# A fused attention and feed-forward kernel: the exponents' matmuls at the end of a step, and the transposes of y behind the last of them

## What is computed

```python
x = x + xattn(layernorm(x), ctx, ctx, Wq, bq, Wk, bk, Wv, bv)   # softmax attention on the context
x = x + attn(layernorm(x), Wq, Wk, Wv, Wo, W_feat)              # causal linear attention, 16 heads of 64
x = x + ffn(layernorm(x), w1, w2)                               # quantised linear, gelu, quantised linear

# attn: phi(v) = exp(v @ W_feat - |v|^2/2) / sqrt(128), 128 features
# y_t = sum_{s<=t} (phi(q_t).phi(k_s)) v_s / (sum_{s<=t} phi(q_t).phi(k_s) + 1e-6);  out = y @ Wo
# ffn: activations are rounded to 8 bits by row, weights to -1, 0, 1
```

## Time and profile before

| | us |
|---|---|
| median of 3 runs | 253.53 |
| lowest and highest | 253.51, 253.79 |
| the profiled execution | 253.28 |
| its span, first to last instruction | 251.5 |
| TensorE busy in the span | 239.7 |
| VectorE busy | 187.6 |
| ScalarE busy | 146.5 |
| GpSimd busy | 101.6 |

### The profile page before, as it was taken

The page is one execution under the profiler, slowest core; times in us unless marked ns, Lnnn a source line. Parts: engine busy times, 40 slices in busy tenths (PEclk is TensorE's granted clock), DMA queues, the critical chain, the costliest instruction groups (busy, mean ns, idle before and its releaser), DMA issues.

```text
span 251.5 us, 6988 instructions
## 1 busy us (share of the span) xinstructions
PE 239.7 (95%) x2722; PEld 188.8 (75%) x2728; DVE 187.6 (75%) x476; ACT 146.5 (58%) x284; POOL 101.6 (40%) x139
## 2 busy tenths in 40 slices
PE   7998889999999999999999999999999989999984
PEld 7854556777788778787777878777789978888863
DVE  5577888666742685777888888775688979999994
ACT  0554454534446888567656766765647257787772
POOL 2063113342202558344674578726720024444430
PEclk9999999999999999999999999999999999999999
DMA  7999999990079001100110000000000000000001
GB/s 189 357 390 404 398 395 393 344 390 33 1 252 330 4 0 46 44 3 1 44 44 3 1 3 3 3 0 3 4 3 3 4 0 3 21 23 21 22 26 63
DMA packets 15377, 26.83 MB, mean 107 GB/s; under 512 B 1232, under 2 KB 8688, under 8 KB 15344
## 3 DMA queue, kind: packets, MB, share of 16 engines
q1 hardware_dynamic: 14576, 25.96, 28.9%
q10 hardware_dynamic: 768, 0.43, 0.6%
HBM read 25.33 MB, written 1.05 MB: 105 GB/s over the span
## 4 chain that ended last, share of the span: by engine, by line
PE 63%; DVE 18%; issue 6%; POOL 5%; ACT 4%; DMA 2%; SPq 0%; DVEq 0%; POOLq 0%; ACTq 0%
PE b L1346 11%; PE b L1106 7%; PE b L1390 6%; PE b L1108 6%; PE b L1107 6%; PE b L1365 4%; PE b L1267 3%; PE b L1270 2%; PE b L1263 2%; DMA xwk<-in_xWk 2%; PE b L1520 2%; DVE yT_lo L980 2%; DVE xn L742 2%; PE b L1218 2%; PE b L1186 2%
## 5 line engine op out<-in xcount | busy, mean ns | idle before, releaser
L852 DVE TENSOR_TENSOR x_lo<-b,x_hi 128x512 fp32r<-128x512 f32 x32 | 21.7, 688 | 16.8 <-ACT x_hi L463 16.7
L600 ACT ACTIVATE phi<-b 128x512 f32<-128x512 f32 x48 | 26.0, 597 | 11.3 <-PE b L1346 11.3
L403 POOL TENSOR_TENSOR sq_lo<-sq_sum,sq_hi 128x512 fp32r<-128x512 f32 x16 | 20.6, 1287 | 25.8 <-ACT sq_hi L463 25.8
L345 POOL TENSOR_TENSOR lnr<-lnv,mh 128x1 f32<-128x1 f32 x16 | 8.8, 552 | 54.9 <-DVE lnv L716 54.7
L521 ACT ACTIVATE sq<-b 128x512 f32<-128x512 f32 x32 | 19.3, 603 | 18.1 <-PE b L1108 18.1
L397 POOL TENSOR_TENSOR sq_sum<-sq,sq 128x512 f32<-128x512 f32 x16 | 20.7, 1293 | 21.6 <-ACT sq L521 21.6
L1106 PE MATMUL b<-nT_lo,wp_hi 128*128 128x512 f32 x64 | 26.8, 418 | 0.1
L1108 PE MATMUL b<-nT_hi,wp_hi 128*128 128x512 f32 x64 | 25.0, 391 | 0.0
L1107 PE MATMUL b<-nT_hi,wp_lo 128*128 128x512 f32 x64 | 25.0, 390 | 0.0
L926 DVE TENSOR_TENSOR smk<-b,mask 64x512 f32<-64x512 f32 x32 | 22.0, 688 | 2.9 <-PE b L1365 1.2
L1390 PEld LDWEIGHTS b<-va,smk 128*64 128x64 f32 x512 | 17.5, 137 | 7.5 <-issue 7.1
(11 more groups left out here) (180 smaller groups left out, 615.9 us busy)
## 6 DMA issues: line engine op xcount, KB each, us to landing
cT<-in_ctxT SPq DMA_DIRECT2D x8, 1028.0 KB, 14.0
cn<-in_ctx SPq DMA_DIRECT2D x8, 1024.0 KB, 14.7
wv_raw<-in_aWv SPq DMA_DIRECT2D x1, 1024.0 KB, 13.8
wp_raw<-in_aWq SPq DMA_DIRECT2D x4, 256.0 KB, 4.0
wp_raw<-in_aWk SPq DMA_DIRECT2D x4, 256.0 KB, 4.2
w_raw<-in_w2T SPq DMA_DIRECT2D x1, 1024.0 KB, 5.4
wo<-in_aWo SPq DMA_DIRECT2D x1, 1024.0 KB, 7.9
w_raw<-in_w1T SPq DMA_DIRECT2D x1, 1024.0 KB, 5.0
```

The costliest lines, as they stand in the source:

```text
L403: nc.gpsimd.tensor_tensor(sq_lo[n % 2][:], sq_sum[:], sq_hi[n % 2][:].bitcast(F32), ALU.subtract).then_inc(sq_l, 1)
L600: nc.scalar.activation(phi(n, a)[:], feature_bank(a), ACT.Exp).then_inc(f_exp, 1)
L852: nc.vector.tensor_tensor(x_lo[n % 2][r][:], proj_bank(n, r), x_hi[n % 2][r][:].bitcast(F32), ALU.subtract).then_inc(x_l, 1)
```

## The change

From step 3 on, exponents(n-1) go behind slot(n), that is, to the end of the step on TensorE. On VectorE outputs(2u-2) go from behind low(n, 1) to between low(n, 0) and low(n, 1) (in step 4 behind weight_scales). In the end of the loop, TensorE's order becomes numerators 24 to 27, exponents(15), the transposes of y of group 0, attention(14), the transpose yTt(1, 0), the first half of project_out(0), attention(15), numerators 28 and 29, its second half, numerators 30 and 31. ScalarE's copies yT_hi of group 0 go between the exponentials of step 15, and the load of the Gelu table behind these. VectorE's yT_lo of group 0 goes ahead of masked(14). attention(14) writes its scores to bank b3 where it was b2. A wait for all exponentials ahead of the output loop goes; ScalarE's loop is not changed.

```diff
         def score_bank(u):
-            return {13: b0[:], 14: b2[:], 15: b4}.get(u, b6)
+            return {13: b0[:], 14: b3[:], 15: b4}.get(u, b6)
...  (ScalarE, behind the loop)
-            features(STEPS - 1, 0, 1, 2, 3)
...
-            nc.scalar.activation(spare[:], mh[:, 0:2], ACT.Gelu)
+            features(STEPS - 1, 0, 1)
             yTc(0, 0)
             yTc(0, 1)
+            features(STEPS - 1, 2, 3)
+            nc.scalar.activation(spare[:], mh[:, 0:2], ACT.Gelu)
...  (VectorE)
                 low(n, 0)
                 if n == 4:
                     weight_scales()
+                u = n - 3
+                if u >= 1:
+                    outputs(2 * u - 2)
                 low(n, 1)
...
-                u = n - 3
-                if u >= 1:
-                    outputs(2 * u - 2)
                 if u >= 0:
                     masked(u)
...
             for v in range(24, 28):
                 outputs(v)
-            masked(14)
             yTc(0, 0)
             yTc(0, 1)
+            masked(14)
             masked(15)
...  (TensorE)
-                exponents(n - 1)
                 if n >= 3:
                     slot(n)
+                exponents(n - 1)
...
-            numerators(24)
-            numerators(25)
+            for v in range(24, 28):
+                numerators(v)
             exponents(STEPS - 1)
-            numerators(26)
-            numerators(27)
-            attention(14)
             yTt(0, 0)
             yTt(0, 1)
-            attention(15)
-            numerators(28)
-            numerators(29)
+            attention(14)
...  (in project_out)
                     if g == 0 and c == 4:
-                        numerators(30)
-                        numerators(31)
+                        attention(15)
+                        numerators(28)
+                        numerators(29)
...
                 mm.then_inc(o_mm, 1)
+                if g == 0:
+                    numerators(30)
+                    numerators(31)
...
-            pe.wait_ge(f_exp, 4 * STEPS)
```

## The result

| | before | after |
|---|---|---|
| median of 4 runs, us | 253.52 | 265.29 |
| ratio, 95% interval | | 1.048 (1.043 to 1.053) |
| span of the profiled execution, us | 251.5 | 263.6 |
| step starts apart, steps 5 to 14, us | 7.335 | 7.99 |

The kernel is 4.8% slower; the forecast was 264.6 us, 4.4% more.

What follows compares the result with a forecast made beforehand. TensorE bounds the kernel before; after the change a ring through ScalarE and VectorE was to bound the loop. Loop +8.8 us and end +2.5 us, +11.3 on 253.28, gave 264.6 us, range 260.5 to 268.0.

Steps and rivals of the forecast that it cites:

- The ring: Loop: exponents, ScalarE's queue, x_lo and outputs on VectorE, second numerators, next exponents; 7.94 us a step against 7.335.
- Numerators to exponents: Loop, TensorE: from the start of 16 numerator matmuls to the exponents directly behind them, 0.58 us.
- Rival 3: Loop, TensorE: the change of shape costs 0.3 us more in each of 12 steps, 268.2 us; chance 0.07.
- Steps 3, 4 and 15: Loop's special steps: exponentials 1.08 us later in 3; 4 +2.2 us through weight_scales; 15 0.64 us over the ring.
- The end: From numerators(24) to the second group's output projection: 16.7 us instead of 14.2, +2.5 us.
- The wait for sq_lo: End: exponents(15) come only four numerators after exponents(14) and wait for sq_lo(15), +0.9 us.
- the transposes' waits: End: scores(14) wait for exponentials of step 15, the next transposes for yT_lo; +0.4 us together.
- The third term: End: numerators 30 and 31 stand behind the first output projection, leaving their outputs uncovered, +1.2 us.
- some tenths for masked(15): End, VectorE: masked(15) now waits for scores inside the first output projection, some tenths of a us.
- The rest: From the second output projection on: VectorE's list and order unchanged, so the last 52 us stay.
- Rival 1: Loop: ring not closed, y in time, 0.21 us wait gone; 253.3 us, or 250.8 with a free end; chance 0.07.

Runs made afterwards that it cites:

- e1: Kernel after, with x_hi's first half copied twice on ScalarE from step 4 on: 272.79 us.
- e2: Kernel before, with x_hi's first half copied twice on ScalarE from step 4 on: 254.6 us.
- e5: Kernel after, with VectorE's loop in its old order (outputs behind both halves of x_lo): 276.47 us.
- e6: Kernel after, with squares_high(n) ahead of all four exponentials of step n-1 on ScalarE from step 3 on: 258.03 us.
- e3: Kernel before, with only the new loop order on TensorE and VectorE, its end as it was: 265.74 us.
- e9: Kernel after, with numerators 30 and 31 three quarters into the first output projection instead of behind it: 264.75 us.
- e12: Kernel after, with attention(15) and numerators 28 and 29 ahead of the first output projection, numerators 30 and 31 in its middle: 264.44 us.
- e7: e6, with squares(n+1, 0) and its x_hi also moved between the two pairs of exponentials on ScalarE: 256.29 us.
- e8: Kernel before, with a step's first numerators moved between the projection and the exponents on TensorE: 252.6 us, 0.996 of before.
- e10: Kernel after, with three of the four weight_scales operations in step 4 moved behind the masks on VectorE: 264.6 us.

## Why the prediction was right, and where it was off

By its own steps:

- **The ring.** Forecast 3.59 + 1.57 + 0.58 + 2.20 = 7.94 us. Measured: 3.59 (146.53 to 150.12), 1.57 (150.12 to 151.69), 0.61, 2.21; the steps are 7.99 apart. All four pieces could be read in the trace of before, two of them at places where the queue had, by accident, the order to come. The mechanism is shown by e1 and e2, e5 and e6, each of which changed one member.
- **Numerators to exponents** was taken as 0.58 us from one row and measured 0.61 to 0.64. This is the only term that was short in each step by more than 0.01 us, and makes up for most of the 0.5 us by which steps 5 to 14 came out longer. Rival 3, a price of 0.3 us for that change of shape, did not come: no gap stands before L1346 in the kernel after. By the Trainium skill (TensorEngine Tiling (Array Packing), the key property that mode switching requires a drain) each change of mode drains TensorE; the gaps of 0.35 us behind the 512-column matmuls agree with it, and behind the 65-column ones the runs show none of that size.
- **Steps 3, 4 and 15.** First exponential of step 2 to that of step 3: forecast 9.92 us, measured 9.94. Step 15: 8.58 and 8.57. That step 4 fits to 0.02 us is in part luck. The 2.58 us from x_lo to the next operation, which the prediction took from the kernel before, held a pair of operations that took 1.80 us there. It took 1.84 in the kernel after, but 0.68 in e3, whose order in step 4 is the same, and there the step was 1.0 us shorter.
- **The end.** 16.7 us forecast, 16.83 measured, but not all by the terms given. The wait for sq_lo was 1.1 us (forecast 0.9), the transposes' waits 0.37 and 0.15 (0.4). The third term, 1.2 us "uncovered" because numerators 30 and 31 come late, had the right size and the wrong cause: e9 undid just that and got 0.23 us. What the prediction listed last, "some tenths for masked(15)", is the larger one: e12, which undid both, got 1.04. So that the end's sum fits is luck.
- **The rest** was forecast to stay, and took 51.9 us in both kernels.
- **Rival 1** was priced wrongly, though it did not decide. It said that without the ring the 0.21 us wait would go too, for a step of 7.1 us. e7 opened the ring, and the wait stayed at 0.20: numerators to y to the next numerators is a way of its own (1.69 us in the earlier trace rows, from 145.61 to 147.30) against 1.48 us of first numerators and scores on TensorE. The step of TensorE's own is 7.3 us in this order; e8 shows what takes the wait away, namely other work between the two numerators.

## What to carry to other kernels

When a block of work is moved to the end of a step on one engine, follow who waits for it through the other engines' queues back to that engine, and add the pieces: if the sum exceeds the engine's own step, that sum is the new step, however idle each engine looks. The queue to add up is the one behind the moved block, in the other engine's unchanged order; look for a place in the trace where that queue already runs back to back, and the sum needs no guess. To take away a short wait for a reader of a shared bank, put independent work between the two writers, not a different neighbour behind both.

## What the runs showed of the hardware

One pair of tiny VectorE operations gave an unexpected microsecond. L834 (two operations on 128x2 elements) in step 4, in the kernel after and in e3, with GpSimd's sq_sum beside it:

```profile
101.08 1.84 DVE L834 TENSOR_SCALAR wsum<-wsum 128x2 f32<-128x2 f32 x2
101.62 1.27 POOL L397 TENSOR_TENSOR sq_sum<-sq,sq 128x512 f32<-128x512 f32 x1
```

```profile
102.88 0.68 DVE L834 TENSOR_SCALAR wsum<-wsum 128x2 f32<-128x2 f32 x2
103.42 1.27 POOL L397 TENSOR_TENSOR sq_sum<-sq,sq 128x512 f32<-128x512 f32 x1
```

In both runs sq_sum starts 0.54 us behind the pair. In the first L834 ends with sq_sum (102.92 and 102.89), in the second it ends 0.14 us after sq_sum's start, and 0.10 us after the GpSimd operation ahead of sq_sum (wp_lo, 102.05 to 103.46). So the second operation of the pair either stood behind sq_sum for its whole length or went ahead of it. What decides this is smaller than the traces resolve. It was worth 1.1 us there, and 1.0 us of the kernel's time, since step 4 has the pair in its path.

e10 has the same pair behind the masks (it is L836 there), 1.8 us after sq_sum has ended and with no other GpSimd operation beside it:

```profile
101.74 1.28 POOL L397 TENSOR_TENSOR sq_sum<-sq,sq 128x512 f32<-128x512 f32 x1
104.81 0.23 DVE L836 TENSOR_SCALAR wsum<-wsum 128x2 f32<-128x2 f32 x2
```

Alone it takes 0.23 us. In e1, e2 and e6 it started while sq_sum was running, and took 1.28, 1.21 and 1.03 us: each time it ended 0.09 to 0.11 us after sq_sum, whatever the start. The Trainium skill (SBUF — State Buffer, the section on who interferes with whom) tells of a pair of ports that VectorE, in the modes that use two ports and that it says tensor_scalar can enter, and GpSimd take for a whole instruction, the other one being fully blocked. These traces agree, with 0.23 us alone and up to 1.84 us beside GpSimd. No run changes GpSimd's side; the cause rests on the pair's times in these traces.

The fall of TensorE's clock in e5 is the other thing: 1.0 us in one of twelve steps, in a kernel whose TensorE was busy for some four fifths of the loop. In the loop of the other kernels whose traces are read here it did not fall. That the waiting brought it about is not shown, since e5's other steps waited as long and kept the full clock.
